# A two-layer graph network on one core: ScalarE copies the gather indices instead of GpSimd, and one wait of ScalarE is moved

## The reference

```python
xn = layernorm(x)
x  = x + gat(xn, src, dst) + linear_attention(xn)      # layer 0, "edges0" computes gat's edge part
x  = x + layernorm(moe_ffn(layernorm(x)) + layernorm(x))   # "ffn0", two experts of 512 hidden features
xn = layernorm(x)
x  = x + tensor_product_conv(xn, node_vec1, src, dst, edge_attr_4, edge_attr_8) \
       + linear_attention(xn)                          # layer 1, "edges1" computes the conv's edge part
x  = x + top_k_ffn(layernorm(x))                       # "ffn1"

# the edge part of gat, 4 heads of 64 channels
e   = leaky_relu(a_src[src] + a_dst[dst], 0.2)
out = segment_sum(h[src] * softmax_over_dst(e)[:, :, None], dst)
# the edge part of the conv
y0, y1 = lin1(xn) * node_vec1                          # one row of 256 numbers for each node
w   = silu(edge_attr_8 @ fc_w1) @ fc_w2
agg = segment_sum(products(w, y[src], edge_attr_4), dst)
```

## Time and profile before

| | |
|---|---|
| median of 3 runs | 3345.35 us (3344.71 to 3345.83) |
| the profiled execution's own time | 3341.32 us |
| its span, first to last instruction | 3339.6 us |
| mean granted TensorE clock | 0.917 of full speed |
| busy share of the span | PE 84%, PEld 64%, DVE 68%, ACT 39%, POOL 59% |
| first to last gather of edges0 | 110.35 to 1175.61 us, 835 DMAs |
| ffn0, first to last instruction | about 1376 to 1775 us |
| first to last gather of edges1 | 1795.34 to 2935.81 us, 834 DMAs |

### The profile page before, as it was taken

The page is one execution under the profiler, slowest core; times in us unless marked ns, Lnnn a source line. Parts: engine busy times, 40 slices in busy tenths (PEclk is TensorE's granted clock), DMA queues, the critical chain, the costliest instruction groups (busy, mean ns, idle before and its releaser), DMA issues. The chain is left out here.

```text
span 3339.6 us, 78237 instructions
## 1 busy us (share of the span) xinstructions
PE 2808.7 (84%) x21943; PEld 2141.9 (64%) x21943; DVE 2282.9 (68%) x6620; ACT 1311.4 (39%) x4384; POOL 1983.1 (59%) x2317
## 2 busy tenths in 40 slices
PE   6677777777777788699997899999999999889399
PEld 4566666666666666588884455555555555568387
DVE  5577777777777777476665677777777777768522
ACT  5333333333333246333332344444444444248122
POOL 3577777777777711011114787787787877722254
PEclk9788888888888899899997899999999999999599
DMA  6544444444444457422223333333333333437221
GB/s 190 164 112 110 111 114 111 112 110 111 114 110 114 127 148 197 139 80 87 82 83 105 103 108 106 107 107 106 107 106 106 107 106 106 120 112 203 58 52 47
DMA packets 239081, 375.71 MB, mean 113 GB/s; under 512 B 88190, under 2 KB 145606, under 8 KB 238762
## 3 DMA queue, kind: packets, MB, share of 16 engines
q0 software_dynamic: 89712, 230.26, 25.1%
q1 hardware_dynamic: 147482, 140.83, 15.0%
q10 hardware_dynamic: 1696, 2.62, 0.2%
HBM read 310.75 MB, written 62.84 MB: 112 GB/s over the span
## 5 line engine op out<-in xcount | busy, mean ns | idle before, releaser
L596 POOL DMA_INDIRECT e_rows<-tab,e_ix x830 | 790.1, 952 | 234.6 <-issue 203.0
L2029 POOL DMA_INDIRECT e_rows<-tab,e_ix x828 | 792.3, 957 | 227.5 <-issue 202.6
L1020 PE MATMUL e_pU<-e_ohp,e_rows 128*128 128x128 f32 x3340 | 518.8, 323 | 5.0 <-DVE e_ohp L868 4.9
L1020 PEld LDWEIGHTS e_pU<-e_ohp,e_rows 128*128 128x128 f32 x3340 | 483.4, 232 | 23.8 <-issue 6.8
L2195 DVE TENSOR_TENSOR e_msg<-e_pW,e_rows 128x384 f32<-128x384 f32 x834 | 422.1, 548 | 0.0
L2259 PE MATMUL e_pU<-e_msg,e_oh 128*32 128x128 f32 (+1 forms) x6672 | 371.7, 310 | 11.3 <-DVE sum L2155 11.0
L2245 PE MATMUL e_pW<-e_w,e_hT 64*128 64x256 f32 x1668 | 317.2, 431 | 43.2 <-DVE e_msg L2195 37.6
L2193 DVE TENSOR_TENSOR e_msg<-e_pW,e_rows 128x256 f32<-128x256 f32 x417 | 175.5, 421 | 250.1 <-PE e_pW L2245 200.7
L705 ACT COPY e_ohT<-e_pT 64x640 bf16<-64x640 bf16 x167 | 114.6, 686 | 546.7 <-PE e_pT L1001 516.5
L2259 PEld LDWEIGHTS e_pU<-e_msg,e_oh 128*32 128x32 f32 x6672 | 243.1, 112 | 132.3 <-issue 71.9
L1001 PE MATMUL e_pT<-e_identB,e_oh 128*64 128x128 bf16 x835 | 86.3, 242 | 248.2 <-DVE e_oh L494 224.3
(11 more groups left out here) (458 smaller groups left out, 5394.8 us busy)
## 6 DMA issues: line engine op xcount, KB each, us to landing
e_rows<-tab,e_ix POOLq DMA_INDIRECT x1658
xnT<-f_xnT SPq DMA_DIRECT2D x25, 250.0 KB, 3.0
e_xk<-xnT SPq DMA_DIRECT2D x25, 250.0 KB
xnT<-b_xT SPq DMA_DIRECT2D x25, 250.0 KB, 2.9
m_xnT<-xnT SPq DMA_DIRECT2D x25, 250.0 KB
xnT<-m_xT SPq DMA_DIRECT2D x25, 250.0 KB, 2.6
ffn_norm<-xnT SPq DMA_DIRECT2D x25, 250.0 KB
tab<-f_hrow SPq DMA_DIRECT2D x25, 227.5 KB
```

What stands on the lines that cost most here:

```text
L596: nc.gpsimd.indirect_dma_start(out=rows[:, s, j, :], out_offset=None, in_=env["tab0"], in_offset=bass.IndirectOffsetOnAxis(ap=at[:, j:j + ...
L1020: nc.tensor.matmul(pU[:, s % 2, 2 * W * k:2 * W * (k + 1)], rows[:, s, j, 128 * k:128 * k + 128], ohp[:, s % 3, j, 2 * k:2 * k + 2, :], st ...
L2029: nc.gpsimd.indirect_dma_start(out=rows[:, r % PER, j, :], out_offset=None, in_=env["tab1"], in_offset=bass.IndirectOffsetOnAxis(ap=at[:, ...
```

## The change

ScalarE now copies the indices, several groups ahead, and GpSimd copies none. In edges0 `ix` becomes a ring of six tiles: ACT's step g copies the indices of group g+6, between its two exponentials, for g from 0 to 155. POOL uses the ring inside the loop (150 groups), where it waits for the copy made six groups earlier; in the unrolled groups it reads its indices straight from `srcI`. In edges1 the ring has ten tiles, and ACT's step g copies the indices of group g+9 between `copied` and `silu`, for g from 1 to 125; POOL uses it in the 110 groups of the loop. In ffn0 ACT's wait for `s_lin` moves from ahead of the first gelu into `rows`, ahead of the first scaling.

```diff
 edges0
-        ix = sb("ix", [P, 2, GT], I32)
+        ix = sb("ix", [P, SLOTS, GT], I32)
...
 edges0, POOL
                     def step(g, s, lo, hi, k):
-                        at = ix[:, s % 2, :] if lo >= 1 else srcI[:, 0:GT]
-                        if lo >= 1:
-                            pool.wait_ge(s_ix, g)
+                        at = ix[:, s, :] if k is not None else srcI[:, g * GT:g * GT + GT]
+                        if k is not None:
+                            pool.wait_ge(s_ix, g - SLOTS + 1)
                         if lo >= SLOTS:
                             hold(pool, s_acc, g - SLOTS + 1)
                         for j in range(GT):
                             if lo >= 1:
                                 for i in ((j,) if j < 3 else range(3, GT) if j == 3 else ()):
                                     hold(pool, s_row[i], 16 * g)
-                            if j == 3 and hi <= GROUPS - 2:
-                                nc.gpsimd.tensor_copy(ix[:, (s + 1) % 2, :], srcI[:, bass.ds((g + 1) * GT, GT)])\
-                                  .then_inc(s_ix, 1)
                             nc.gpsimd.indirect_dma_start(
...
 edges0, ACT
                         nc.scalar.activation(p[:, s % 3, :, :], ee[:, 4 + s % 2, :, :], ACT.Exp)
+                        if hi < LATE:
+                            nc.scalar.copy(ix[:, s, :], srcI[:, bass.ds((g + SLOTS) * GT, GT)]).then_inc(s_ix, 1)
                         nc.scalar.activation(pp[:, s % 3, :, 0:H0], ee[:, 4 + s % 2, :, :], ACT.Exp).then_inc(s_p, 1)
...
 ffn0, ACT
                 act.wait_ge(s_b1, 32)
-                act.wait_ge(s_lin, 96)
 
                 def rows(u, s, lo):
                     if lo >= 2:
                         hold(act, s_sr[s], (u // 2) * 32)
                     hold(act, s_Y, u + 1)
+                    if lo == 0:
+                        act.wait_ge(s_lin, 96)
...
 edges1
-        ix = sb("ix", [P, 2, T1], I32)
+        ix = sb("ix", [P, 2 * PER, T1], I32)
...
 edges1, POOL
-                        at = ix[:, r % 2, :] if lo >= 1 else srcI[:, 0:T1]
-                        if lo >= 1:
-                            pool.wait_ge(s_ix, g)
+                        at = ix[:, r, :] if lo < hi else srcI[:, g * T1:g * T1 + T1]
+                        if lo < hi:
+                            pool.wait_ge(s_ix, g - 2 * PER + 1)
...
-                            if j == 3 and hi <= GROUPS1 - 2:
-                                nc.gpsimd.tensor_copy(ix[:, (r + 1) % 2, :], srcI[:, bass.ds((g + 1) * T1, T1)])\
-                                  .then_inc(s_ix, 1)
...
 edges1, ACT
                         if lo >= 1:
                             copied(g - 1, lo - 1)
+                        if lo >= 1 and hi <= LAST:
+                            nc.scalar.copy(ix[:, (r - 1) % (2 * PER), :], srcI[:, bass.ds((g + 2 * PER - 1) * T1, T1)])\
+                              .then_inc(s_ix, 1)
                         if hi <= GROUPS1 - 2:
                             silu(g + 1, r + 1, lo + 1)
```

## The result

| | us, median | lowest to highest | executions |
|---|---|---|---|
| before | 3345.59 | 3344.71 to 3346.80 | 4 |
| changed | 3311.47 | 3308.41 to 3315.48 | 4 |

The ratio is 0.9898 (95% interval 0.9881 to 0.9916): 34.1 us less. The forecast was 3312.5. The profiled execution of the changed kernel was the slowest of its four, 3315.48 us (span 3313.7).

What follows compares the result with a forecast made beforehand. POOL's gathers were taken to bound both edge stages; 13.9 (edges0) + 12.1 (edges1) + 6.8 (ffn0) = 32.8 us off the median 3345.35 gave 3312.5 us, chance 0.84, range 3306 to 3324.

Steps and rivals of the forecast that it cites:

- POOL sets the pace of both edge stages: Edges0 and edges1: POOL is saturated by gathers 1.25 us from start to start, and the other engines follow.
- 0.09 a copy: Edge stages: an index copy costs POOL 0.06 us ahead of the next gather and 0.03 through that longer gather.
- The first rival: Edge stages: only the copy's 0.06 us leaves, the longer gather coming from semaphore waits; 24.2 us in all, 3321.1; chance 0.08.
- a tail of 0.30 that covers the copy: POOL, edge stages: 0.30 us behind each gather is its tail, in which most of the 0.19 us copy lies.
- edges0, 13.9 us: Edges0: groups 0 to 153 each lose a copy of 0.09 us; 15.0 if the last twelve counted too.
- edges1, 12.1 us: Edges1: groups 0 to 128 lose a copy of 0.09 us each, 11.6, plus 0.5 for the 50 behind a power.
- gathers of 0.95 at 1.25 from start to start everywhere but at powers and the long gaps: Expected sign in the profile after, POOL's gathers in both edge stages, with no copy left on POOL.
- A distance above 1.25: Edge stages: a sign that the prediction is wrong, the distance of gathers growing above 1.25 us.
- ffn0, 6.8 us: Start of ffn0: 3.8 us of idle PE leave, and 2.95 from chunk 1's hidden layer at full clock.
- ACT's copy, priced 0.20 and hidden: Edge stages: each index copy takes ACT 0.20 us, on no path that sets the end.
- What is late next: DVE's wait for rows in edges0 falls from 0.51 to 0.42 us, ACT's for scales from 3.3 to about 3.0.
- The long gaps: Edges0: some eight gathers with unexplained longer gaps, left as they are; at most 9 us come or go with the copies.

Runs made afterwards that it cites:

- e6: Kernel before with a second, useless copy on POOL just ahead of each index copy: 3374.62 us, ratio 1.0089.
- e11: Changed kernel plus a useless copy on POOL where the index copy stood, and the next group's wait for it: 3331.87 us against 3338.92 of the kernel before.
- e5: Changed kernel without ACT's index copies, looped groups all gathering by the first group's indices: 3312.03 us against 3346.27 of the kernel before.
- e8: Changed kernel with seven more, useless copies on ACT behind each index copy: 3312.99 us, ratio 0.9904 to the kernel before.
- e3: Kernel before with only the edges1 part of the change: 3334.31 us, ratio 0.9968.
- e12: Changed kernel with edges1's inverse square roots moved from POOL to ACT and DVE: 3264.52 us against 3338.92 of the kernel before.
- e1: Kernel before with only the ffn0 part, the moved wait: 3341.97 us, ratio 0.9987.
- e7: Kernel before with 16 useless matmuls on PE behind chunk 0's hidden layer in ffn0, all waits kept: 3352.98 us in one execution.
- e2: Kernel before with only the edges0 part of the change: 3329.56 us, ratio 0.9953.
- e4: The changed kernel once more, against the kernel before: 3314.29 us, ratio 0.9907.
- e9: Changed kernel plus a useless copy on POOL where the index copy stood, on a slow chip: 4292.56 us against 4291.91 of the kernel before.
- e10: Changed kernel with edges1's inverse square roots moved from POOL to ACT and DVE, on a slow chip: 4357.07 us, ratio 1.015 to the kernel before.

## Why the prediction was right

- **POOL sets the pace of both edge stages**: right. A copy more on POOL lengthens them (e6), a copy put back restores them (e11), and no copy on any other engine matters (e5, e8).
- **0.09 a copy**: right in size. In edges0 of the kernel before the means are 1.309 from a gather to the next across a copy (162 places) and 1.282 from there to the one after, against 1.250. e11 has 1.309 and 1.282 with a copy of no use. The first rival, that the longer gather comes from the waits, falls: the changed kernel's gathers keep the group's waits and are 0.95. The reason given was wrong, a tail of 0.30 that covers the copy. By it e6 should have lost twice what it did.
- **edges0, 13.9 us**: too small by a little. Among rows at 1.250 it is 1091.0 with the copies (mean of before, e3, e11) and 1076.0 without (e5, e12), so 15.0. Among those at 1.253 it is 1095.5 (e1, e7) and 1078.8 (changed, e2, e4, e8), so 16.7. First to last gather it is 16.0 and 16.6, somewhat above 166 x 0.09 = 14.9. So the copies of the last twelve groups seem to have counted too, while in e6 3.8 of 17.1 us were lost in that tail. With rows of one kind 2 us apart, and the last copies never varied by themselves, what sets the end stays open.
- **edges1, 12.1 us**: too large. It is 10.1 at 1.250 (1168.0 to 1158.0) and 10.5 at 1.253 (1171.0 to 1160.5). First to last gather it is 10.5 in both. The step that failed is "gathers of 0.95 at 1.25 from start to start everywhere but at powers and the long gaps". The copies cost what was worked out, but the 732 plain gathers left moved apart, 1.2523 to 1.2551, which gives 2.0 us back, and 12.1 less 2.0 is what the stages show. A distance above 1.25 was one of the prediction's signs of being wrong; it came, 0.003 large. The longer distance is in all of them. In the kernel before it sat in one stretch of each five groups, behind the first of the two powers (1.261), and ended with the next group's copy; the others were at 1.250. Why it spreads when the copies go is open. It goes back to that stretch when they return (e11), ACT's copies are not the cause (e5), and without the powers it is 1.250 again (e12).
- **ffn0, 6.8 us**: right in both halves. The idle 3.82 is gone, chunk 1 runs at a granted clock of 1.00, and against the 33.7 us of the kernel before 6.6 to 7.1 leave in every profile with the hunk. e7 shows the clock half by itself.
- **ACT's copy, priced 0.20 and hidden**: hidden, yes, and without table loads. It is 0.18 to 0.20 long, but adds only 0.08 to 0.09. No gather waited for it (the one that the profile lists has the same gap without it).
- **What is late next**: half right. DVE's wait for rows went from 0.51 to 0.46 a group, not 0.42. ACT's wait for the scales did not shrink to 3.0 but is 3.4. That number can't carry a difference of 0.3: it is 3.1, 3.2, 3.3 and 3.3 in four profiles with the same edges1 (e7, e1, e2, before), 3.4 to 3.5 in changed, e4 and e3, and 2.9 without ACT's copies (e5) but 3.0 with eight of them (e8). The conclusion, that neither wait reaches zero, held.
- **The long gaps**: neither came nor went in sum. Beside the distances above, 6.7 us in edges0 before and 6.2 after. The 550th, 659th and 768th gather have one in both, so they do not hang on the copies; what they are is open.
- The sum by stages is 15 to 17, 10 and 7: 32 to 34, with 32.8 forecast. Edges0's error and edges1's cancel, which is luck, and so is that the total came about 1 us from the forecast; the mechanism was right but for the two steps named, the 0.30 taken for a tail and the gathers' distance taken as fixed.

## What to carry to other kernels

An engine can be the bottleneck at a 59% busy share: read the distance of its starts, not its busy time, and ask whether anything but itself ends its gaps. Price a small instruction by how far it moves the starts behind it (0.09 us here for one copy on POOL, 0.115 more for a second, each 0.19 long), and moving it to an engine with idle time is then worth that much times its count, if it is issued far enough ahead. A wait that stops PE at the start of a dense stage costs its idle time and then the slower clock behind it.

## What was unexpected

- The 0.30 us ahead of a gather reads as the gather's own start. Small work ahead of it is partly free, but not because it fills a tail: it costs 0.060 for the first copy, 0.115 for the second.
- The same gathers come 1.250 us apart in one profiled execution (before, e3) and 1.253 in another (e1, e7), throughout; e1 and e3 ran on one chip. Over 1669 gathers that is some 5 us, nearly as large as ffn0's term, so traces are compared stage by stage and at the same distance. Whether it belongs to a build or to an execution is open.
- POOL's gathers showed no sign of a lock by other engines' work. The Trainium skill (SBUF — State Buffer, section "SBUF: two separate sides") tells of one between DVE and GpSimd; no gather here was longer than 1.02 us on the mean at any place of the five-group cycle, and those at 1.02 stand behind a power. No run varied DVE's work.
- One chip ran the kernel before at 4292 us instead of 3339 to 3346. In the two kernels profiled there (e9, e10) the time is lost in the edge stages alone, with POOL's and DVE's instructions of the same length and long stalls between them; PE's matmuls were longer (`e_pKV` in edges1 841 ns against 622, at a mean granted clock of 0.83 against 0.92). There a gain on POOL was worth nothing.
